# Cross-attention and a routed expert block on one core: GpSimd's copy of token numbers moved ahead of the norm, and three VectorE operations of the routing merged away

## The reference, cut to what matters

```python
x = x + xattn(layernorm(x), ctx, ctx)           # one head, softmax over 120 keys
h = layernorm(x)                                # 4096 rows of 256
logits = h @ Wr.T + br                          # 8 experts
topk_vals, topk_idx = top_k(logits, 2)
topk_w = softmax(topk_vals)
for e in range(8):
    cw = sum(topk_w * (topk_idx == e), axis=-1)
    y = gelu(h @ W1[e].T + b1[e]) @ W2[e].T + b2[e]     # 256 -> 1024 -> 256
    out = out + cw[:, None] * y
z = out + h
x = x + layernorm(z) * ln_w + ln_b
```

## Time and profile before

| | us |
|---|---|
| median of 3 runs | 652.23 |
| lowest, highest | 650.58, 652.34 |
| profiled execution, its own time | 648.82 |
| its span, first to last instruction | 646.9 |
| busy: TensorE matmul | 558.2 (86%) |
| busy: VectorE | 427.6 (66%) |
| busy: GpSimd | 350.5 (54%) |
| busy: ScalarE | 282.9 (44%) |

### The profile page before, as it was taken

One profiled execution on the slowest core, in us unless ns is written; L12 is line 12 of the kernel. 1 busy time (PEld: TensorE's weight loads), 2 busy tenths in 40 slices (PEclk: granted clock), 3 DMA queues, 4 the chain that ended last, 5 costly groups with the idle time before them and its releaser, 6 DMA issues.

```text
span 646.9 us, 17861 instructions
## 1 busy us (share of the span) xinstructions
PE 558.2 (86%) x4922; PEld 497.7 (77%) x4923; DVE 427.6 (66%) x1292; ACT 282.9 (44%) x723; POOL 350.5 (54%) x464
## 2 busy tenths in 40 slices
PE   6999989996578999999999999999999999997000
PEld 5899889885457898989898989898898988775000
DVE  1688888887735576666757575757575766445494
ACT  3687777775334434333333333343434243331142
POOL 4027666677741464656465555565555545542397
PEclk8999999998559999999999999999999999999555
DMA  7756566755432342323232322223232323221753
GB/s 256 245 168 209 185 201 214 214 182 167 144 100 44 37 51 50 49 49 49 49 48 49 47 50 42 55 41 56 41 57 40 56 29 48 43 37 24 226 171 130
DMA packets 64387, 63.92 MB, mean 99 GB/s; under 512 B 15656, under 2 KB 59632, under 8 KB 63952
## 3 DMA queue, kind: packets, MB, share of 16 engines
q1 hardware_dynamic: 48672, 44.34, 22.0%
q0 software_dynamic: 15680, 19.15, 18.0%
HBM read 38.82 MB, written 24.64 MB: 98 GB/s over the span
## 4 chain that ended last, share of the span: by engine, by line
PE 66%; POOL 10%; DVE 8%; issue 7%; DMA 7%; ACT 1%; POOLq 1%; DVEq 0%; SPq 0%; ACTq 0%
PE bank L829 11%; PE bank L831 10%; PE bank L830 10%; PE bank L851 10%; PE bank L853 9%; PE bank L852 9%; POOL slot_table L563 6%; DMA slot_table<-rows_now,slots 4%; PE bank L808 2%; DVE w1hi L1303 2%; DVE w2lo L1290 2%; POOL rn L539 1%; DMA z_rows<-xn,sidx 1%; PE bank L747 1%; DVE st L1085 1%
## 5 line engine op out<-in xcount | busy, mean ns | idle before, releaser
L989 ACT ACTIVATE stage<-bank,b1s 128x256 f32<-128x256 f32 (+1 forms) x312 | 125.0, 452 | 178.6 <-PE bank L831 137.7
L598 POOL DMA_INDIRECT z_rows<-xn,sidx x71 | 114.3, 1609 | 145.8 <-DVE xn L1237 120.1
L829 PE MATMUL bank<-xnt,w1hi 128*128 128x256 f16 (+1 forms) x624 | 164.4, 265 | 7.0 <-issue 3.5
L830 PE MATMUL bank<-xnt,w1hi 128*128 128x256 f16 (+1 forms) x624 | 163.7, 264 | 0.0
L831 PE MATMUL bank<-xnt,w1lo 128*128 128x256 f16 (+1 forms) x624 | 163.6, 264 | 0.0
L851 PE MATMUL bank<-w2hi,stage 128*128 x568 | 154.9, 273 | 2.6 <-DVE xn L1237 2.4
L1218 DVE CAST stage<-stage 128x512 f16<-128x512 f32 (+1 forms) x156 | 75.2, 482 | 121.3 <-PE bank L853 121.1
L852 PE MATMUL bank<-w2lo,stage 128*128 x568 | 154.8, 273 | 0.0
L853 PE MATMUL bank<-w2hi,stage 128*128 x568 | 154.8, 273 | 0.0
L1220 DVE TENSOR_TENSOR stage<-stage 128x512 f16<-128x512 f32 (+1 forms) x156 | 102.3, 656 | 5.4
L580 POOL DMA_INDIRECT xn<-tokens_dram,gidx x71 | 73.2, 1032 | 43.9 <-PE bank L808 26.5
(11 more groups left out here) (167 smaller groups left out, 865.6 us busy)
## 6 DMA issues: line engine op xcount, KB each, us to landing
stage<-in_L_ffn_W_dram SPq DMA_DIRECT2D x16, 768.0 KB, 5.3
x<-in_x_dram SPq DMA_DIRECT2D x16, 256.0 KB
tokens_dram<-xn SPq DMA_DIRECT2D x16, 256.0 KB
z_rows<-xn SPq DMA_DIRECT2D x16, 256.0 KB
stage<-in_L_ffn_W_dram SPq DMA_DIRECT2D x16, 256.0 KB, 3.7
w1hi<-z_rows SPq DMA_DIRECT2D x8, 512.0 KB, 7.7
out_dram<-w2hi SPq DMA_DIRECT2D x8, 512.0 KB, 2.9
slot_table<-w1lo SPq DMA_DIRECT2D x2, 1024.0 KB, 10.0
```

The lines of the kernel that those rows point to most:

```text
L598: nc.gpsimd.indirect_dma_start(out=z_rows, out_offset=bass.IndirectOffsetOnAxis(ap=sidx[p][:, t:t + 1], axis=0), in_=y_sb[p][:, t, :], in_ ...
L829: nc.tensor.matmul(dst, w1hi[:, col], xhi[:, k, 0:bt], start=(k == 0), stop=False)
L830: nc.tensor.matmul(dst, w1hi[:, col], xlo[:, k, 0:bt], start=False, stop=False)
L989: ins = nc.scalar.activation(h32[:, c * bt:(c + 1) * bt], f_h[q][:, (c % 2) * bt:(c % 2 + 1) * bt], ACT.Gelu, bias=b1s[p][:, c:c + 1], sca ...
```

## The change

GpSimd's copy of the token numbers, with its wait for `published`, moves to the front of GpSimd's step, ahead of the norm. The wait for `leads_ready` and the semaphore go; of the waits before the scatters, those for the copy and for `slots_ready` stay. On VectorE the two subtractions of the leads become one with a reversed operand; the reduction of the slot numbers writes integers itself, so that the conversion L1113 goes, and stands ahead of the first `low_part`; the comparison that makes the one-hot table reads the integer indices and an integer `iota8`, so that the conversion L1150 goes. Both VectorE counters go by four a step in place of five.

```diff
--- before.py
+++ after.py
@@ -104,7 +104,7 @@
         ones = sb("ones", [P, P])
         before = sb("before", [P, P], BF16)
         ones_bf = sb("ones_bf", [P, P], BF16)
-        iota8 = sb("iota8", [P, E])
+        iota8 = sb("iota8", [P, E], U32)
         slot0 = sb("slot0", [P, E])
         minus_half = sb("minus_half", [P, 2, TJ])
         ids = sb("ids", [P, NT * TOPK, 2], I32)
@@ -163,13 +163,11 @@
         lg = sb("lg", [P, TJ, E])
         mx = sb("mx", [P, TJ, E])
         ix = sb("ix", [P, TJ, E], U32)
-        ixf = sb("ixf", [P, TJ, TOPK])
         oh = sb("oh", [P, TJ, TOPK, E])
         chosen = sb("chosen", [P, TJ, E], BF16)
         seen = sb("seen", [P, E], BF16)
         slot_e = sb("slot_e", [P, TJ, E])
         prod = sb("prod", [P, TJ, TOPK, E])
-        slotf = sb("slotf", [P, TJ * TOPK])
         slots = [sb(f"slots{i}", [P, TJ * TOPK], I32) for i in range(2)]
         rows_now = [sb(f"rows_now{i}", [P, TJ * TOPK, LINE], I32) for i in range(2)]
         leads = [rows_now[i][:, :, 2].bitcast(F32).rearrange("p (j k) -> p j k", k=TOPK) for i in range(2)]
@@ -293,7 +291,6 @@
         wlo_ready = sem("wlo_ready")
         count_mm = sem("count_mm")
         blocks_ready = sem("blocks_ready")
-        leads_ready = sem("leads_ready")
         tanh_ready = sem("tanh_ready")
         gates_ready = sem("gates_ready")
         y_raw = sem("y_raw")
@@ -511,7 +508,7 @@
                                     pattern=[[-1, P]], channel_multiplier=1)
             nc.gpsimd.affine_select(out=before[:, :], in_=before[:, :], compare_op=ALU.is_gt, fill=0.0, base=0,
                                     pattern=[[1, P]], channel_multiplier=-1)
-            nc.gpsimd.iota(iota8[:, :], [[1, E]], base=0, channel_multiplier=0, allow_small_or_imprecise_dtypes=True)
+            nc.gpsimd.iota(iota8[:, :], [[1, E]], base=0, channel_multiplier=0)
             nc.gpsimd.iota(slot0[:, :], [[TOK, E]], base=0, channel_multiplier=0, allow_small_or_imprecise_dtypes=True)
             nc.gpsimd.iota(jota[:, 0:FULL], [[TB, FULL]], base=0, channel_multiplier=0, allow_small_or_imprecise_dtypes=True)
             nc.gpsimd.iota(jota[:, FULL:], [[1, SHORT]], base=0, channel_multiplier=0, allow_small_or_imprecise_dtypes=True)
@@ -541,6 +538,12 @@
                 nc.gpsimd.tensor_tensor(shift, nmu, scale, ALU.mult).then_inc(ready, 1)
 
             def step(t, u, measure, project, attend, renorm, route, publish):
+                if publish is not None:
+                    m, p = publish
+                    b = 2 * m + p
+                    n = TJ * TOPK
+                    at_least(pool, published[p], ROUTED * m)
+                    nc.gpsimd.tensor_copy(rows_now[p][:, :, 0:2], ids[:, bass.ds(b * n, n), :]).then_inc(rows_copied, 1)
                 if measure is not None or renorm is not None:
                     w = slice(0 if measure is not None else 1, 2 if renorm is not None else 1)
                     at_least(pool, xn_ready, min(t - 1, NB) if isinstance(t, int) else t - 1)
@@ -549,15 +552,9 @@
                     norm(t, mv[u][:, w, :, 0], mv[u][:, w, :, 1], nmu[u][:, w, :], ve[u][:, w, :], minus_half[:, w, :],
                          rn[u][:, w, 0, :], rn[u][:, w, 1, :], EPS_LN, rn_ready)
                 if publish is not None:
-                    m, p = publish
-                    b = 2 * m + p
-                    n = TJ * TOPK
                     if isinstance(b, int) and b == 0:
                         pool.wait_ge(table_blank, 16 * PADS)
-                    at_least(pool, published[p], ROUTED * m)
-                    nc.gpsimd.tensor_copy(rows_now[p][:, :, 0:2], ids[:, bass.ds(b * n, n), :]).then_inc(rows_copied, 1)
                     pool.wait_ge(rows_copied, b + 1)
-                    alone(pool, leads_ready, b + 1, tally_pool)
                     alone(pool, slots_ready, b + 1, tally_pool)
                     for a in range(n):
                         nc.gpsimd.indirect_dma_start(
@@ -775,7 +772,7 @@
                 transpose_group(t, project, 1)
                 if route is not None:
                     pe.wait_ge(xn2t_ready, r + 1)
-                    at_least(pe, slot_self, 5 * r - 4)
+                    at_least(pe, slot_self, 4 * r - 3)
                     for j in range(TJ):
                         for k in range(KD):
                             ins = nc.tensor.matmul(b_lg[:, j, :], xn2t[:, k, j * P:(j + 1) * P], wrt[:, k, :],
@@ -1091,7 +1088,7 @@
                     dve.wait_ge(chosen_ready, k + 1)
                     nc.vector.tensor_tensor(seen[:, :], seen[:, :], chosen[:, 0, :], ALU.add).then_inc(slot_self, 1)
                 if publish is not None:
-                    dve.wait_ge(slot_self, 5 * k + 2)
+                    dve.wait_ge(slot_self, 4 * k + 2)
                     nc.vector.tensor_tensor(seen[:, :], seen[:, :], chosen[:, 1, :], ALU.add).then_inc(seen_ready, 1)
                     for j in range(TJ):
                         ins = nc.vector.tensor_tensor(prod[:, j, :, :], oh[:, j, :, :],
@@ -1104,13 +1101,11 @@
                             ins = nc.vector.bn_aggr(mv[u][:, w, j, :], st[u][:, w, j, :])
                     ins.then_inc(stats_ready, 1)
                 if publish is not None:
-                    dve.wait_ge(slot_self, 5 * k + 4)
-                    nc.vector.tensor_reduce(slotf[:, :], prod[:, :, :, :].rearrange("p j k e -> p (j k) e"), AX.X, ALU.add).then_inc(slot_self, 1)
+                    dve.wait_ge(slot_self, 4 * k + 4)
+                    at_least(dve, published[pk], ROUTED * mk)
+                    with nc.allow_low_precision(reason="a sum of one slot number and zeros"):
+                        nc.vector.tensor_reduce(slots[pk][:, :], prod[:, :, :, :].rearrange("p j k e -> p (j k) e"), AX.X, ALU.add).then_inc(slots_ready, 1)
                 low_part(t, project, 0)
-                if publish is not None:
-                    at_least(dve, published[pk], ROUTED * mk)
-                    dve.wait_ge(slot_self, 5 * k + 5)
-                    nc.vector.tensor_copy(slots[pk][:, :], slotf[:, :]).then_inc(slots_ready, 1)
                 if project is not None:
                     dve.wait_ge(v_mm, b + 1)
                     if isinstance(b, int) and b == 0:
@@ -1127,7 +1122,7 @@
                     nc.vector.tensor_tensor(lg[:, :, :], b_lg, br_bc[:, :].unsqueeze(1).to_broadcast([P, TJ, E]), ALU.add).then_inc(top_self, 1)
                 low_part(t, project, 1)
                 if route is not None:
-                    alone(dve, top_self, 5 * r + 1, tally_dve)
+                    alone(dve, top_self, 4 * r + 1, tally_dve)
                     for j in range(TJ):
                         ins = nc.vector.max(mx[:, j, :], lg[:, j, :])
                     ins.then_inc(top_self, 1)
@@ -1139,24 +1134,21 @@
                                                              in1=rows_of(a, j), op0=ALU.mult, op1=ALU.add)
                     ins.then_inc(x1_ready, 1)
                 if route is not None:
-                    alone(dve, top_self, 5 * r + 2, tally_dve)
+                    alone(dve, top_self, 4 * r + 2, tally_dve)
                     for j in range(TJ):
                         ins = nc.vector.max_index(ix[:, j, :], mx[:, j, :], lg[:, j, :])
                     ins.then_inc(top_self, 1)
                     at_least(dve, published[pr], ROUTED * mr)
-                    nc.vector.tensor_tensor(leads[pr][:, :, 0], mx[:, :, 0], mx[:, :, 1], ALU.subtract)
-                    nc.vector.tensor_tensor(leads[pr][:, :, 1], mx[:, :, 1], mx[:, :, 0], ALU.subtract).then_inc(leads_ready, 1)
-                    dve.wait_ge(top_self, 5 * r + 3)
-                    nc.vector.tensor_copy(ixf[:, :, :], ix[:, :, 0:TOPK]).then_inc(top_self, 1)
+                    nc.vector.tensor_tensor(leads[pr], mx[:, :, 0:TOPK], mx[:, :, 1::-1], ALU.subtract)
                 low_part(t, project, 2)
                 if route is not None:
-                    dve.wait_ge(top_self, 5 * r + 4)
-                    nc.vector.tensor_tensor(oh[:, :, :, :].rearrange("p j k e -> p (j k) e"),
-                                            iota8[:, :].unsqueeze(1).to_broadcast([P, TJ * TOPK, E]),
-                                            ixf[:, :, :].rearrange("p j k -> p (j k)").unsqueeze(2).to_broadcast([P, TJ * TOPK, E]),
+                    dve.wait_ge(top_self, 4 * r + 3)
+                    nc.vector.tensor_tensor(oh[:, :, :, :],
+                                            iota8[:, :].unsqueeze(1).unsqueeze(1).to_broadcast([P, TJ, TOPK, E]),
+                                            ix[:, :, 0:TOPK].unsqueeze(3).to_broadcast([P, TJ, TOPK, E]),
                                             ALU.is_equal).then_inc(top_self, 1)
                 if route is not None:
-                    dve.wait_ge(top_self, 5 * r + 5)
+                    dve.wait_ge(top_self, 4 * r + 4)
```

## The result

The changed kernel takes 647.12 us (median of 10 runs, 642.77 to 650.97) where the kernel before, run beside it, takes 651.75 (650.13 to 652.34): a ratio of 0.9937 [0.9911, 0.9964], so 4.1 us less by the ratio, with an interval of 2.3 to 5.8. The forecast was 3.0 us less. Two further comparisons, on two different chips, gave 0.9947 and 0.9954; the mean of the three is 0.9946, 3.5 us.

The account below looks back on a forecast made before the run. No engine was full in the batch loop; a chain of waits bound it. Gains of 0.26, 0.68, 0.4, 0.49, 0.28, 0.63 and 0.24 us make 3.0: 652.23 - 3.0 = 649.2 us, range 645.2 to 651.6.

Parts of the forecast that it names:

- The bound: Expert stage: TensorE is full and untouched, so only an earlier start counts; a microsecond gained in the batch loop is one saved.
- The gap: GpSimd, from the norm's last operation to the first scatter: 0.86 us in place of 1.35, a gain of 0.49.
- rival B: GpSimd's gap does not shrink by overlap; first scatter 0.77 us after the norm's last operation ends; 650.3 to 651.0 us; chance 0.28.
- The copy ahead of the norm: GpSimd: idle time covers the copy in even steps; 0.20 us charged in odd steps and wherever GpSimd is the bound.
- C: Rival, loop and tail: the copy delays the norm and all that hangs on it; +2.5 us, 654.7; chance 0.07.
- The contention that the prediction left out: GpSimd's copy beside VectorE's two-input operations: up to 0.25 us in each of 14 steps by the rule; nothing added.
- The landing tied to SyncE's loads: Steps 6 to 13: scatters land behind SyncE's loads, tied to the norm; a shorter gap gains nothing unless a scatter overtakes.
- Rival A: Loop: each landing follows its scatter, 0.66 us in each of four steps; 4.5 us in all, 647.7; chance 0.20.
- The overtaking: Steps 8, 10 and 12: the fourth scatter gets ahead of the x load; 0.4 us counted of 1.1.
- VectorE: Subtraction of the leads before the next weight part: 0.17 us at four landings, steps 6, 8, 10, 12; 0.68 us.
- The tail: Steps 16 to 18, GpSimd the bound: 0.21 us each, 0.63; steps 19 and 20: 0.12 each, 0.24.
- The sum: Whole kernel: the gains of steps 5 to 20 together make 3.0 us, giving 649.2 us against the median.

Follow-up runs that it names:

- copy back: The changed kernel with GpSimd's copy put back behind the norm, all else kept: 647.46 us, 0.9968 of before; 0.9959 on a third chip.
- VectorE part: The changed kernel with GpSimd's step put back as before: 648.91 us, 0.9998 of before; 0.9952 on a third chip.
- whole change: The changed kernel run once more, unaltered, against the kernel before: 646.09 us, ratio 0.9947; its three traces include the first measurement and a later rerun.
- GpSimd part: The kernel before with the copy ahead of the norm and no wait for leads_ready: 648.55 us, 0.9973 of before; 0.9995 on a third chip.
- waits early: The changed kernel with GpSimd's waits before the scatters put between the norm's power and product: 645.04 us, 0.9921 of before; 1.0114 on a third chip.
- whole change run again: The changed kernel, unaltered, run on another chip against the kernel before: 647.74 us, ratio 0.9954.
- first experiments: Whole change, GpSimd part, VectorE part and weights last, run on one chip against the kernel before, which took 649.98 us there.
- weights last: The changed kernel with SyncE's weight load put behind the next step's row loads: 647.24 us, 0.9961 of before.

## Why the prediction was right, point by point

- **The bound.** Right. The change moved the start of the expert stage; TensorE's busy time in it is unchanged (299.65 of 300 us).
- **The gap.** Forecast 0.86 us, measured 0.85 and 0.86 in steps 12 and 13 and 0.78 in steps 16 to 18: the 0.8 us is counted from the wait, and rival B, by which it was to start only at L538's end (0.20 + 0.77 = 0.97), falls. The copy back shows the split, 0.10 for the wait and 0.39 for the copy.
- **The copy ahead of the norm.** Right in the tail: the periods of steps 17 and 18 fell from 7.65 and 7.64 to 7.39 and 7.36, by 0.27 and 0.28; forecast 0.21. In the loop I feared 0.20 in each odd step and charged it only where GpSimd was the bound; step 13's found 0.81 us of idle time. C falls. The contention that the prediction left out is too small to matter: the one copy that ran beside both operations of VectorE's pair L1094, at 71.99, is the longest of the 16, 232 ns, and the copy's median rose from 188 to 200 ns; L1094 itself took a mean of 169 ns in place of 170. That is 0.01 to 0.04 us in place of the bound of 0.25.
- **The landing tied to SyncE's loads.** Right, and the step on which the sum hung. Counted from the start of the norm's last operation, the scatters of steps 6 and 8 to 13 landed after 10.67 us in the mean before, 10.66 with the VectorE part and 10.62 with the copy back; after 10.51, 10.63 and 10.54 in the three traces of the whole change and 10.57 with the GpSimd part, though their scatters start 0.4 to 0.5 us sooner. So the shorter gap brought the landings 0.0 to 0.2 us forward. In single steps it went both ways: in steps 9, 11 and 13 the landing got longer by more than the scatter got earlier, 5.29 to 6.11, 5.05 to 6.56 and 5.19 to 6.16 us. Rival A, in which every landing follows its scatter, falls, and moving the weights moved the landing. With the waits early, another 0.5 us sooner, the same mean is 9.65: there the scatters did gain on the loads.
- **The overtaking.** Right in kind, in another step, and in part luck. Step 7 shows what it hangs on. In after, the last scatter's issue ends at 71.98 and the x load is issued at 72.26, since the weight load ahead of it held SyncE for 1.60 us; the landing took 3.26 us in place of 6.21. In the whole change run again the weight load's issue took 0.39 us there, the x load came at 74.78, ahead of the scatter's end at 75.71, and the landing took 6.37 us (SyncE's queue of both, below). Before it had taken 1.06 us, and the x load's issue ended 0.35 us ahead of the scatter's. The x load came 5.96 us after the norm's last operation in after, 5.74 in the second trace (landing 4.63 us), 4.76 in the third, the scatter always at the same place: the change brought the scatter 0.5 us forward, SyncE's own timing, which the change doesn't touch, did the rest. I had looked for the overtaking in steps 8 to 12 at 0.4 us; it came in step 7, and the next pair gained from it (the period from step 8 to 9 fell from 9.48 to 7.97, and is 9.09 in the whole change run again). Of the 1.7 us that the stretch is longer in that run, 1.1 are these, and 0.8 are step 18, where GpSimd waited 0.90 us for VectorE's statistics.

```profile
70.43 1.60 SPq L399 DMA_DIRECT2D stage<-in_L_ffn_W_dram  x1
72.26 0.40 SPq L385 DMA_DIRECT2D x<-in_x_dram  x1
```
```profile
74.16 0.39 SPq L399 DMA_DIRECT2D stage<-in_L_ffn_W_dram  x1
74.78 0.44 SPq L385 DMA_DIRECT2D x<-in_x_dram  x1
```

- **VectorE.** Mis-sized: 0.17 us for each landing on the chain, measured 0.34 - 0.23 = 0.11, so 0.4 for the four and not 0.68. The error was to read the price of the operation that is left from the distance behind L1150, 0.17 us, the last of three that run close behind each other (their starts lie 0.07 and 0.09 us apart); a lone subtraction has 0.23 us to the weight part. The integer forms cost nothing: the comparison took 182 ns in place of 184 (medians), the reduction a mean of 159 in place of 156. Alone this part shows no gain in time on the chip of the first experiments (0.9998).
- **The tail.** Steps 16 to 20 gave 0.85 us, forecast 0.63 + 0.24 = 0.87; 1.02 and 0.19 in the other two traces. Steps 19 and 20 gave 0.08 to 0.09 each where 0.12 was forecast, 16 to 18 together 0.69 where it was 0.63. Step 15 lost 0.33, gained 0.12 and lost 0.16; forecast was a gain of 0.28. Step 14 gained 0.88, 0.44 and 0.87; forecast 0.49.
- **The sum.** Step 5's gap gave 0.44 us, forecast 0.46. The stretch behind it gave 3.10, 2.99 and 1.38 us in the three traces of the whole change, a mean of 2.5; the forecast was 3.0 - 0.46 = 2.54. Within it steps 6 to 13 gave 1.70, 1.43 and 0.48, where the terms make 0.68 + 0.4 - 0.20 = 0.88. That the mean meets the forecast so closely is partly luck: single traces differ by 1.7 us, and there is one of before. The first matmul of the experts came at 184.95, not 186.7; of the 1.75 us between, 0.80 lay ahead of all that the change touches, 0.56 is what this trace's stretch gave beyond the forecast, and 0.38 came between the last scatter and the experts. "Nothing changed behind it" holds for the work, but not for a single trace: the stage took 2.9 us longer, with more of it at half clock.
- **A rule on the queues.** That each DMA engine takes turns between its queue rows, packet by packet (the Trainium skill, DMA: Bandwidth & Descriptors, Queues, rings and completion order) does not fit as a forecast here: by it the place of the weight load should hardly matter to the scatters, and moving it took their landing from 4.6 to 6.6 us in the whole change's traces, step 7 of after aside, down to 3.3 to 4.9. Whether a held scatter already stood in its queue, no row tells.

The measured 4.1 us lies 1.1 above the forecast, which is inside the measured interval; the mean of three comparisons, 3.5, is nearer. Part of the gain hangs on a race of the scatters with the x load that single executions win or lose, and of the two parts only GpSimd's shows a gain of time on its own there (0.9973, just clear of its interval).

## What to carry to other kernels

An indirect DMA behind a separate waiting instruction on GpSimd started some 0.8 us after that wait in all rows here (0.77 to 0.84), also where what it waited for was long there. So try the waits where an operation of the engine still runs behind them (here under the power, 0.36 us instead of 0.86), and short copies where the engine idles; but measure the kernel, since the same edit went with 0.9921 on one chip and 1.0114 on another. When a transfer's landing stands in the chain, look first at what stands ahead of it in the order of arrival: an earlier issue was worth next to nothing here until it got past a load, and moving the load moved the wait to the engine that needs it.

## What was not expected of the hardware

- Landings of one and the same scatter took 2.1 us at the end of the loop without other traffic, 3.3 to 4.9 us with the weights last, 3.5 to 3.8 with the waits early as well, and mostly 5 to 6.6 us behind a load.
- The expert stage, equal in all kernels, took 404.84 to 409.44 us. In the GpSimd part's trace the clock was back at full speed when the experts started, and the first block took 7.72 us in place of after's 10.63. Its windows:

```profile
186.00:188.00 2.00, 0.52 (x6) 0.46 (x6) 0.69 (x1) 0.59 (x1) 1.05 (x2) 0.96 0.22 66
188.00:190.00 2.00, 2.00 (x20) 1.80 (x19) 0.00 (x0) 0.84 (x2) 0.94 (x1) 1.00 0.72 219
```

- The same kernel before took 649.98 and 650.48 us on two chips and 665.65 on a third, where in each loop step ScalarE and VectorE wait up to 1.9 us (VectorE part) for signals that the profile puts down to nothing it knows; the early waits gain on the second and lose on the third.
